# Layer-0 feed-forward finished batch by batch, and the causal maxima of layer 1 split between two stages

## The chip, the cores and the metric

One core of one Trainium2 chip runs the whole kernel as one launch. The metric is the device time of that launch in microseconds (us). Engines: PE is TensorE, DVE is VectorE, ACT is ScalarE, POOL is GpSimd, SP is SyncE, which here issues DMAs.

## The reference

Two transformer layers on x of 2 batches x 512 rows x 256 columns, all in float32. Each layer is

```python
h = layernorm(x) * (1 + ca) + sa
x = x + ga * attention(h)
h = layernorm(x) * (1 + cb) + sb
x = x + gb * ffn(h)
```

where the shifts, scales and gates are `silu(c) @ wmod`, per batch. Layer 0 has local attention (16 heads of 16, each query sees the 64 keys before it and itself) and a feed-forward part of one shared expert and 16 routed ones (top 4 of two groups). Layer 1 has causal attention:

```python
q = (h @ Wq.T + bq)            # 16 heads of 16
k = h @ Wk.T + bk              # one head of keys and of values for all
v = h @ Wv.T + bv
scores = where(k_pos < q_pos, q k^T / 4, NEG_BIG)
out = softmax(scores) @ v @ Wo.T + bo
```

and a feed-forward part of a shared expert of 1024 and 8 routed ones (top 2).

## The kernel before

**Arithmetic.** Every float32 product that needs the precision is made of float32r passes: an operand is split in a high part (ACT copies it to float32r) and a low part (DVE or POOL subtracts), and PE multiplies high x high, low x high and high x low (`product`, L553).

**Layer-0 feed-forward.** The hidden width is cut in 25 tiles of 128. A *unit* is one tile for one batch, 50 units in all. A unit is an up product `up` (L553: two halves g and u of six matmuls each, in PSUM banks 4 and 5), silu of g on ACT (L1308), g times u on DVE (L1783), times the routing weight (L1786), the high part on ACT (L1312), the low part on DVE (L1790) and the down product `down` (L994, twelve matmuls into the batch's two banks, 0 and 1 or 2 and 3, which gather the sum over all tiles). PE runs up(u), down(u-1), up(u+1) and so on. Units alternate between the batches, tile by tile, but for the last three tiles (`TAIL`): these are done for batch 0 and then for batch 1. Each tile's weights come by one DMA of 384 KB (`load_ffn`) into one of two raw buffers, ACT makes their high part (L1288), POOL their low part (L519, `weights_low`), into two pairs of tiles, `fwR`.

**Between the layers.** `half_out` (DVE) gates the summed output and adds it to x, with the statistics of the next norm; `norm_scales` and `normalise` follow, eight PE transposes (`norm_transposes`), `modulate` and `h_high` on ACT, `h_low` on DVE. Then `project1(b, m)` gives the queries (m = 0, 1), keys (2) and values (3) of layer 1; ACT adds the bias and makes high parts (`take_q1`), DVE low parts (`q1_low`). For this, `filler` puts matmuls without use into PE's stream (8 + 6 + 6 + 4 of them).

**Causal maxima.** Softmax needs each query's maximum over its keys before the scores are made again the other way round. For each of 32 heads (16 per batch) ACT masks the queries (`mask_q`, L1160), PE makes the scores (`scores`, L724 and the mask L729) in three banks, as three *pieces*, and DVE takes three maxima (`maxima`, L1572). Two groups of three banks alternate. The maxima go to DRAM (`store_maxima`, through SP) and come back as rows of the query operand in `qk_slot` (`load_keys_major`). All 32 heads are done before the next stage; the projections of batch 1 and the gates of layer 1 (`gates1`, L590) stand between the first ones.

**Values.** `keys_major(1, j)`, j = 0 to 47, makes scores with keys as rows for a third of the work of a pair of heads (L846, masks L852 and L855), in one of three pairs of banks; ACT takes the exponential (L1228); `values` (L877) multiplies with the values, one step late by a *quad* of four heads, which is six j; DVE turns and divides the result (`outputs`, L1588 to L1605). `values_pass(1)` runs over both batches without a break; the output projection of batch 0 (L892) stands in quads 5 and 6, and the norm transposes of batch 0 ahead of the last quad's values. The layer-1 feed-forward follows.

The order on each engine is the order of the code; nothing is scheduled by a program.

## Time and profile before

| what | value |
|---|---|
| three runs | 650.33, 648.99, 645.38 us |
| median | 648.99 us |
| span of the profiled execution, first to last instruction | 648.5 us |
| PE, DVE, ACT, POOL busy | 599.5, 379.0, 302.4, 118.5 us |
| mean granted clock of PE | 0.982 of 2.4 GHz |
| chain that ended last | PE 67%, DVE 19%, ACT 6% |

The profiler's execution is told by its span alone; no separate time of it is given. The span lies within 0.1% of the median of the runs, so that a sum made on the span can be read as one on the median. A clock of 1.00 in the rows is the level of 2.4 GHz, 0.50 that of 1.2 GHz; a value in between is a mean over a stretch that has both.

### The profile page before, as it was taken

Reading aid. Unit: us, or ns where it says so; the run is one execution under the profiler, and the core shown is the slowest. Engines: PE = TensorE matmul, PEld = TensorE weight load, DVE = VectorE, ACT = ScalarE, POOL = GpSimd, SP = SyncE. Lnnn points to the kernel's source line nnn. Section 1 sums busy time; section 2 is a strip of 40 time slices with the busy share of each in tenths; the row PEclk is TensorE's granted clock in tenths of the full one; section 3 lists DMA queues with packets and bytes.
Section 4 is the critical chain, followed back from the end, with each engine's and each line's share of the span. In section 5 each row is a group of like instructions: output and inputs, shape, how many; then the busy total and the mean of one; then the engine's idle time right before and its main releaser. Section 6 shows DMA issues by size and latency. Waiting matters only on the chain.

```text
span 648.5 us, 10714 instructions
## 1 busy us (share of the span) xinstructions
PE 599.5 (92%) x3880; PEld 470.2 (73%) x3890; DVE 379.0 (58%) x757; ACT 302.4 (47%) x466; POOL 118.5 (18%) x90
## 2 busy tenths in 40 slices
PE   3899999898999999999999797889999999999995
PEld 3778645786888888888887565544446878888885
DVE  7567757753254544454457799795376543335556
ACT  3666775463233333333342583448855643333331
POOL 4500031223022222112230000001301231222220
PEclk9998999999699999999999899899999999999999
DMA  8454674000011111111100024402310000111101
GB/s 319 123 213 135 221 215 132 1 25 24 2 36 42 45 49 49 49 49 49 49 25 1 0 71 134 127 4 77 113 40 1 25 25 25 50 49 49 48 2 65
DMA packets 22195, 44.66 MB, mean 69 GB/s; under 512 B 3632, under 2 KB 7632, under 8 KB 22160
## 3 DMA queue, kind: packets, MB, share of 16 engines
q1 hardware_dynamic: 21840, 44.05, 21.5%
q8 instruction: 23, 0.38, 0.2%
q10 hardware_dynamic: 320, 0.13, 0.1%
q14 instruction: 12, 0.10, 0.0%
HBM read 33.16 MB, written 11.01 MB: 68 GB/s over the span
## 4 chain that ended last, share of the span: by engine, by line
PE 67%; DVE 19%; ACT 6%; issue 3%; DMA 3%; POOL 1%; SPq 1%; DVEq 0%; ACTq 0%
PE PS L553 32%; PE PS L994 15%; DVE nmx L1572 5%; PE PS L877 4%; DMA qk_slot<-rows_scr 2%; PE PS L846 2%; PE PS L825 2%; PE PS L830 2%; DVE stats L1470 1%; PE PS L724 1%; DVE x L1641 1%; DVE xn L1786 1%; PE PS L892 1%; PE PS L713 1%; PE PS L561 1%
## 5 line engine op out<-in xcount | busy, mean ns | idle before, releaser
L1312 ACT ACTIVATE qk_hi<-xn 128x512 fp32r<-128x512 f32 x82 | 51.7, 631 | 170.5 <-DVE xn L1786 140.8
L553 PE MATMUL PS<-h_hi,wqkv_hi 128*128 128x512 f32 x304 | 104.4, 401 | 2.6 <-DVE h_lo L1504 1.9
L553 PE MATMUL PS<-h_hi,wqkv_lo 128*128 128x512 f32 x272 | 92.3, 395 | 1.8 <-DVE xn L1696 1.8
L1783 DVE TENSOR_TENSOR prs<-prs,PS 128x512 f32<-128x512 f32 x60 | 41.2, 687 | 88.7 <-PE PS L553 77.7
L519 POOL TENSOR_TENSOR wqkv_hi<-fw_raw,wqkv_hi 128x768 fp32r<-128x768 f32 x18 | 33.1, 1841 | 254.3 <-ACT wqkv_hi L1288 254.3
L1790 DVE TENSOR_TENSOR qk_lo<-xn,qk_hi 128x512 fp32r<-128x512 f32 x70 | 48.4, 692 | 49.1 <-ACT qk_hi L1312 49.1
L1308 ACT ACTIVATE prs<-PS 128x512 f32<-128x512 f32 x82 | 48.5, 592 | 47.3 <-PE PS L553 47.3
L553 PEld LDWEIGHTS PS<-h_hi,wqkv_hi 128*128 128x128 f32 x304 | 58.1, 191 | 15.3 <-DVE h_lo L1504 2.7
L553 PE MATMUL PS<-h_lo,wqkv_hi 128*128 128x512 f32 x160 | 63.6, 397 | 0.0
L553 PEld LDWEIGHTS PS<-h_hi,wqkv_lo 128*128 128x128 f32 x272 | 51.1, 188 | 13.3 <-DVE xn L1696 2.7
L1572 DVE TENSOR_REDUCE nmx<-PS 128x512 f32 (+4 forms) x96 | 54.2, 635 | 4.6 <-PE PS L729 4.5
L994 PE MATMUL PS<-wqkv_hi,qk_hi 128*128 128x256 f32 x280 | 52.1, 285 | 0.9 <-POOL qk_lo L525 0.7
L519 POOL TENSOR_TENSOR wqkv_lo<-fw_raw,wqkv_lo 128x768 fp32r<-128x768 f32 x16 | 29.5, 1846 | 122.4 <-ACT wqkv_lo L1288 122.4
L553 PE MATMUL PS<-h_lo,wqkv_lo 128*128 128x512 f32 x128 | 50.3, 393 | 0.0
L994 PEld LDWEIGHTS PS<-wqkv_hi,qk_hi 128*128 128x128 f32 x280 | 45.0, 188 | 5.0 <-POOL qk_lo L525 1.6
L994 PE MATMUL PS<-wqkv_lo,qk_hi 128*128 128x256 f32 x256 | 47.3, 283 | 0.7 <-DVE qk_lo L1790 0.7
L1786 DVE TENSOR_TENSOR xn<-prs,V 128x512 f32<-128x512 f32 x60 | 44.7, 745 | 2.1
L994 PEld LDWEIGHTS PS<-wqkv_lo,qk_hi 128*128 128x128 f32 x256 | 41.0, 188 | 4.0 <-DVE qk_lo L1790 1.5
L994 PE MATMUL PS<-wqkv_hi,qk_lo 128*128 128x256 f32 x140 | 39.5, 282 | 0.0
L1566 DVE TENSOR_REDUCE nmx<-PS 128x384 f32 (+1 forms) x64 | 31.1, 548 | 13.0 <-PE PS L713 12.9
L994 PE MATMUL PS<-wqkv_lo,qk_lo 128*128 128x256 f32 x128 | 36.0, 281 | 0.0
L1160 ACT ACTIVATE q_masked<-qk_hi,headmask 128x512 fp32r<-128x512 f32 (+1 forms) x48 | 32.3, 715 | 5.5 <-PE PS L729 3.5
(259 smaller groups left out, 1203.2 us busy)
## 6 DMA issues: line engine op xcount, KB each, us to landing
fw_raw<-in_ffn SPq DMA_DIRECT2D x41, 384.0 KB, 3.1
qk_slot<-rows_scr SPq DMA_DIRECT2D x32, 200.0 KB
rows_scr<-qk_hi SPq DMA_DIRECT2D x16, 256.0 KB
qk_slot<-q_scr SPq DMA_DIRECT2D x32, 100.0 KB
rows_scr<-qk_lo SPq DMA_DIRECT2D x8, 256.0 KB
wmod<-in_wmod SPq DMA_DIRECT2D x1, 1536.0 KB, 13.4
x<-in_x SPq DMA_DIRECT2D x2, 512.0 KB, 4.1
wmod<-in_wmod SPq DMA_DIRECT2D x1, 1024.0 KB, 9.6
```

The source lines that it names most:

```text
L519: nc.gpsimd.tensor_tensor(w[1], fw[s][:, :], w[0].bitcast(F32), ALU.subtract)\
L553: ins = nc.tensor.matmul(dst, left(a, c), right(b, c), start=n == 0, stop=n == total - 1)
L877: ins = nc.tensor.matmul(PS[s * VW:s * VW + rows, O_BANK[l][g % 2], kb * P:kb * P + n], v, probs[l][slot][:, col:col + n], start=kb == 0, ...
L994: ins = nc.tensor.matmul(PS[:, 2 * b + t // 2, (t % 2) * D:(t % 2 + 1) * D], hidR[u % 2 if isinstance(u, int) else b][a][:, t * P:(t + 1) ...
L1160: nc.scalar.activation(qm[s][:, :], rows[:, bass.ds(head // 2, 1), :].rearrange("p m t -> p (m t)").bitcast(F32), ACT.Copy, scale=headmask ...
L1308: nc.scalar.activation(gact[b], PS[:, 4, :], ACT.Silu).then_inc(f["silu"], 1)
L1312: nc.scalar.activation(hidR[b][0], hid[b], ACT.Copy).then_inc(f["hi"], 1)
L1566: nc.vector.tensor_reduce(nmx[:, bass.ds(NT * u + 2 * i, 2)], PS[:, 2 * h + i, 0:2 * KEYS0].rearrange("p (t k) -> p t k", k=KEYS0), X, ALU ...
L1572: nc.vector.tensor_reduce(nmx[:, bass.ds(NT * u + qt, k)], PS[:, 3 * h + bank, 0:k * w].rearrange("p (t k) -> p t k", k=w), X, ALU.max, ne ...
L1783: tt(hid[buf] if half is None else gu[buf], gact[buf], PS[:, 5, :], ALU.mult).then_inc(f["gu"], 1)
L1786: tt(hid[buf], gu[buf], cB[b][half], ALU.mult).then_inc(f["hid"], 1)
L1790: tt(hidR[buf][1], hid[buf], hidR[buf][0].bitcast(F32), ALU.subtract).then_inc(f["lo"], 1)
```

## The change

1. The layer-0 feed-forward runs its first 18 tiles by alternating batches, then the last seven tiles (`TAIL0`) for batch 0 and then for batch 1. It is written out without a loop. Weights have four pairs of tiles in place of two (and three more for the tail); ACT makes a tile's high part two tiles ahead of its use, right behind the silu of a unit instead of at the unit's end (`SPLIT0`).
2. During batch 1's seven units, batch 0 goes through `half_out`, the norm, the transposes, `modulate`, and its four layer-1 projections. The gates of layer 1 and their DVE steps go to the feed-forward's units 9 to 13. The fillers of this region are gone.
3. The causal maxima of batch 0 stand beside batch 1's norm and projections, with five banks in turn. Of batch 1, four heads (`AHEAD`) follow at once; the other twelve are cut in 36 pieces, two behind each `keys_major(1, j)` for j = 2 to 19 of batch 0's values, in three banks.
4. The values pass runs per batch (`values_pass1`), without overlap between the batches. Its scores have two pairs of banks in place of three (`PAIR_BANK`), so that `keys_major(1, j)` waits for the exponential of j - 2. The second store of maxima moves from ACT's queue to SP's, behind batch 0's loads.
5. The output projection of batch 0 stands at j = 30, its norm transposes at j = 39, `modulate` and `h_high` on ACT behind j = 40.

The core of the diff:

```diff
-TAIL = [3, 2]
+TAIL = 2
+TAIL0 = 7
+LAST0 = 2 * TILES[0]
+APART0 = TILES[0] - TAIL0
+TURN = LAST0 - TAIL0
+SCORE1 = [(0, 1, 6, 4, 5), (2, 3, 7)]
+PAIR_BANK = [0, 4]
+AHEAD = 4
+        fw0R = [fwR[0], fwR[1], fwX, fwE[1]]
...
+        SPLIT0 = {2 * APART0 - 4: APART0, 2 * APART0 - 3: APART0 + 1, 2 * APART0 - 1: APART0 + 2,
+                  **{2 * APART0 + k: APART0 + 2 + k for k in range(1, 5)},
+                  **{2 * i - 4: i for i in range(EARLY + 2, APART0)}}
...
+        def pieces_at(j):
+
+            first = 3 * AHEAD + 2 * (j - 2)
+            return [(n // 3, n % 3) for n in (first, first + 1) if 3 * AHEAD <= n < 3 * H]
...
             sp.wait_ge(ff[0]["split"], TILES[0])
             for s in range(2):
                 load_ffn(1, 0, s, s)
             store_maxima(sp, 1, 0)
-            sp.wait_ge(at[0]["st"], UNITS)
-            load_attention(1)
+            load_attention(1, 0, H)
+            store_maxima(sp, 1, 1)
+            load_attention(1, H, UNITS)
...
-                if u >= THIRDS:
-                    pe.wait_ge(a["p"], u - THIRDS + 1)
+                if u >= 2:
+                    pe.wait_ge(a["p"], u - 1)
+                if u == 0:
+                    pe.wait_ge(k1_loaded, 16 * 4)
+                    pe.wait_ge(a["mxd"], 3 * H)
+                elif u == THIRDS * PAIRS // 2:
+                    pe.wait_ge(k1_loaded, 16 * 4 * B)
+                    pe.wait_ge(a["mxd"], 3 * UNITS)
+                    pe.wait_ge(a["mlo"], B)
...
+            def beside_ffn0(u):
+
+                if u == EU + 1:
+                    pe.wait_ge(cB_ready, HALVES[0] * B)
+                    shifts1()
+                elif u == EU + 3:
+                    pe.wait_ge(shifts1_taken, 1)
+                    gates1(0)
+                    gates1(1)
+                elif u == TURN + 3:
+                    norm_transposes(2, (0,))
+                elif u == TURN + 4:
+                    project1(0, 2)
+                elif u == TURN + 5:
+                    project1(0, 3)
+                    project1(0, 0)
+                elif u == TURN + 6:
+                    project1(0, 1)
+
+            def ffn0():
+
+                early_ffn(0)
+                combine_table(0, 1)
+                for u in range(EU + 1, LAST0):
+                    b, i = unit0(u)
+                    up(0, u, b, weights(0, i), i)
+                    b, i = unit0(u - 1)
+                    down(0, u - 1, (u - 1) % 2, b, weights(0, i))
+                    beside_ffn0(u)
+                down_apart(0, LAST0 - 1, 1, weights(0, TILES[0] - 1))
...
+                    elif u == TURN:
+                        first = half_out(0, 0, 0)
+                        last = half_out(0, 0, 1)
+                    elif u == TURN + 1:
+                        first()
+                        last()
+                        norm_scales(2, slice(0, 1))
+                    elif u == TURN + 4:
+                        h_low(2, 0)
...
+                q1_low(0, 0)
+                first = half_out(0, 1, 0)
+                last = half_out(0, 1, 1)
+                first()
+                last()
+                norm_scales(2, slice(1, B))
+                normalise(2, 1)
+                q1_low(0, 1)
...
+                for i in range(H):
+                    maxima1(1, i)
+                    if i == 9:
+                        outputs(1, 0)
+                    elif i == 13:
+                        outputs(1, 1)
+                max_low(1, 1)
+                outputs(1, 2)
+                outputs(1, 3)
+                add_output_bias()
...
+            def values_pass1(b, beside):
+
+                first = b * THIRDS * PAIRS // 2
+                for j in range(first, first + 6):
+                    keys_major(1, j)
+                    beside(j)
+                for g in range(b * BQ + 1, (b + 1) * BQ):
+                    keys_major(1, 6 * g)
+                    beside(6 * g)
+                    keys_major(1, 6 * g + 1)
+                    beside(6 * g + 1)
+                    for kb in range(NT):
+                        values(1, g - 1, (kb,))
+                        keys_major(1, 6 * g + 2 + kb)
+                        beside(6 * g + 2 + kb)
+                values(1, (b + 1) * BQ - 1, range(NT))
```

How the instructions stand now, at three places. On PE at the end of the layer-0 feed-forward, before: the first row is the low part of the last but one down product, `o_parts` holds batch 0's normalised x, `wkv` the key and value weights.

```order
L1039 MATMUL PS<-qk_hi,qk_lo 128x256 x4
L696 MATMUL PS<-maskB,zeroB 128x512 x8
L631 MATMUL PS<-ident,o_parts 128x128 x8
L1034 MATMUL PS<-q_masked,qk_hi 128x256 x8
L1039 MATMUL PS<-q_masked,qk_lo 128x256 x4
L682 MATMUL PS<-hF,wkv 128x512 x2
L687 MATMUL PS<-wkv,hF 128x16 x8
```

The same place on PE now: from the end of down(47) to the first product of the last unit, whose weights are in `qk_slot` (`wq` are the query weights of layer 1).

```order
L1078 MATMUL PS<-prx_r,qk_lo 128x256
L748 MATMUL PS<-wkv,hF 128x16 x8
L616 MATMUL PS<-h_hi,wq_hi 128x512
L616 MATMUL PS<-h_lo,wq_hi 128x512
L616 MATMUL PS<-h_hi,wq_lo 128x512
L616 MATMUL PS<-h_hi,wq_hi 128x512
L616 MATMUL PS<-h_lo,wq_hi 128x512
L616 MATMUL PS<-h_hi,wq_lo 128x512
L616 MATMUL PS<-h_hi,qk_slot 128x512
```

The value and query projections of batch 0 stand between two units of batch 1; the fillers are gone, and so are the transposes between the last two down products.

On DVE, in the last units of batch 1, now (`h_lo` is batch 0's low part for the layer-1 norm, `wmod_r` its low part of the queries and keys, `V` its values; the last two rows are batch 1's output):

```order
L2009 TENSOR_TENSOR qk_lo<-xn,qk_hi 128x512
L1668 TENSOR_TENSOR h_lo<-hF,h_hi 128x512 x2
L2002 TENSOR_TENSOR prs<-prs,PS 128x512
L2005 TENSOR_TENSOR xn<-prs,V 128x512
L2009 TENSOR_TENSOR qk_lo<-xn,qk_hi 128x512
L1862 TENSOR_TENSOR wmod_r<-w_raw,wmod_r 128x512
L1867 TENSOR_TENSOR V<-PS,bv 128x4x16
L2002 TENSOR_TENSOR prs<-prs,PS 128x512
L2005 TENSOR_TENSOR xn<-prs,V 128x512
L2009 TENSOR_TENSOR qk_lo<-xn,qk_hi 128x512
L1862 TENSOR_TENSOR wmod_r<-w_raw,wmod_r 128x512
L1809 TENSOR_TENSOR xn<-PS,gate 128x512
```

Before, the rows of `h_lo` and the low parts stood behind the last output (L1639) and ahead of the first maximum (L1572); batch 1's output and norm still stand ahead of the first maximum (L1741).

On PE in the values, before, with keys (L846), masks (L855) and values (L877) in turn:

```order
L846 MATMUL PS<-qk_slot,k 128x256 x2
L855 MATMUL PS<-maskB,identB 128x128 x2
L877 MATMUL PS<-prs,V 32x384 x2
L877 MATMUL PS<-prx,V 32x384 x2
L846 MATMUL PS<-qk_slot,k 128x512 x2
L855 MATMUL PS<-maskB,identB 128x128 x2
```

The same place now, in batch 0's pass:

```order
L879 MATMUL PS<-qk_slot,k 128x256 x2
L888 MATMUL PS<-maskB,identB 128x128 x2
L789 MATMUL PS<-wqkv_hi,q_masked 128x256 x2
L794 MATMUL PS<-maskB,identB 128x256
L794 MATMUL PS<-maskB,identB 128x128
L789 MATMUL PS<-wqkv_hi,q_masked 128x384
L794 MATMUL PS<-maskB,identB 128x128
L910 MATMUL PS<-prs,V 32x384 x2
L910 MATMUL PS<-prx,V 32x384 x2
L879 MATMUL PS<-qk_slot,k 128x512 x2
L888 MATMUL PS<-maskB,identB 128x128 x2
```

Two pieces of a head of batch 1 (L789 and its masks) have come between a keys step and the values.

## Rows read from the trace of the kernel before

**Rows 1.** By stretch: busy us (xcount) of PE, PEld, DVE, ACT, POOL; clock; DMA; GB/s.
```profile
360.40:373.30 12.90, 10.76 (x51) 7.18 (x52) 10.32 (x34) 6.52 (x13) 0.00 (x0) 0.87 0.00 0
373.30:410.80 37.50, 33.13 (x210) 24.36 (x209) 37.11 (x67) 18.24 (x29) 0.00 (x0) 1.00 0.36 106
410.80:434.20 23.40, 17.54 (x101) 11.41 (x101) 19.34 (x36) 11.18 (x17) 0.00 (x0) 0.93 0.18 60
434.20:491.80 57.60, 56.58 (x514) 25.41 (x515) 31.06 (x68) 44.44 (x56) 9.39 (x6) 1.00 0.22 66
413.70:417.30 3.60, 3.59 (x14) 2.63 (x14) 2.01 (x4) 2.43 (x4) 0.00 (x0) 0.53 0.23 75
```
**Rows 2.** Waits from 360 to 434 us: total, times, longest.
```profile
PE PS L724 <- DVE nmx L1572: 7.6, 16, 1.0
```
**Rows 3.** Stretch of the maxima, DVE busy with L1572 alone.
```profile
373.30:434.20 60.90, 52.92 (x94) 0.97 0.29 89
```
**Rows 4.** Timeline of PE, first products of two heads in a row.
```profile
418.92 0.50 PE L724 MATMUL PS<-wqkv_hi,q_masked 128*128 128x256 f32 x2 [0.23 <-DVE nmx L1572]
...
420.58 0.50 PE L724 MATMUL PS<-wqkv_hi,q_masked 128*128 128x256 f32 x2 [0.40 <-DVE nmx L1572]
```
**Rows 5.** Chain that ended last, layer-0 feed-forward: start, us, what.
```profile
256.25 2.78 PE PS L553 x12
259.03 1.43 PE PS L994 x12
```
**Rows 6.** Timeline of PE in layer 1's values, two quads apart.
```profile
446.80 1.07 PE L877 MATMUL PS<-wmod,V 128*32 128x512 f32 x8
...
459.98 1.06 PE L877 MATMUL PS<-wmod,V 128*32 128x512 f32 x8
```
**Rows 7.** Timeline of PE at the end of that feed-forward.
```profile
353.70 0.64 PE L1039 MATMUL PS<-qk_hi,qk_lo 128*128 128x256 f32 x4
...
357.93 1.09 PE L631 MATMUL PS<-ident,o_parts 128*128 128x128 f32 x8 [1.84 <-ACT o_parts L1124]
...
359.80 0.64 PE L1039 MATMUL PS<-q_masked,qk_lo 128*128 128x256 f32 x4
```
**Rows 8.** Timeline of PE among the maxima: key and value projection, gates.
```profile
378.22 1.94 PE L682 MATMUL PS<-hF,wkv 128*128 128x512 f32 x4
...
389.91 1.91 PE L687 MATMUL PS<-wkv,hF 128*128 128x16 f32 x16
...
405.14 1.95 PE L590 MATMUL PS<-wmod,o_parts 128*128 128x256 f32 x8
```
**Rows 9.** Timeline of DVE: batch 1's output, batch 0's low parts, batch 1's norm.
```profile
360.48 0.69 DVE L1639 TENSOR_TENSOR xn<-PS,gate 128x512 f32<-128x512 f32 x1 [1.36 <-PE PS L1039]
...
364.99 1.26 DVE L1504 TENSOR_TENSOR h_lo<-hF,h_hi 128x512 fp32r<-128x512 f32 x2
...
368.54 1.38 DVE L1498 TENSOR_SCALAR xn<-x,mv,rs 128x256 f32<-128x256 f32 x4
```
**Rows 10.** Timeline of SP's queue, the store of maxima and the loads behind it.
```profile
412.74 0.57 SPq L304 DMA_DIRECT2D q_scr<-mxT_hi  x1
...
415.25 37.47 SPq L372 DMA_DIRECT2D qk_slot<-q_scr  x20
```
**Rows 11.** Chain that ended last, layer 0: a load of rows behind others.
```profile
74.61 7.86 DMA qk_slot<-rows_scr
```
**Rows 12.** Timeline of ACT: modulation of batch 0 and its high parts.
```profile
490.72 1.43 ACT L1134 ACTIVATE hF<-PS,modT 128x512 f32<-128x512 f32 x2
492.05 1.14 ACT L1141 ACTIVATE h_hi<-hF 128x512 fp32r<-128x512 f32 x2
```
**Rows 13.** Timeline of PE: batch 1's last output projection in layer 1.
```profile
498.12 0.39 PE L892 MATMUL PS<-wout_hi,qk_hi 128*128 128x256 f32 x1 [1.01 <-POOL qk_lo L496]
```
**Rows 14.** Timelines of POOL, DVE and PE around 327 us: one weight split.
```profile
327.13 1.85 POOL L519 TENSOR_TENSOR qk_lo<-fw_raw,qk_hi 128x768 fp32r<-128x768 f32 x1
...
327.27 2.26 DVE L1786 TENSOR_TENSOR xn<-prs,V 128x512 f32<-128x512 f32 x1
...
330.98 0.51 PE L994 MATMUL PS<-wqkv_lo,qk_hi 128*128 128x256 f32 x2 [0.32 <-DVE qk_lo L1790]
```

More of the change, by code:

```diff
@@ new lines, in up @@
+            def up(l, u, b, w, tile, halves=(0, 1)):
+                f = ff[l]
+                ge(f["split"], tile + 1)
+                for i in halves:
+                    if i == 0:
+                        ge(f["silu"], u)
+                    elif isinstance(u, int) and u <= EU:
+                        ge(f["early_hid"], u)
+                    else:
+                        ge(f["gu"], u - EU)
+                    product(PS[:, 4 + i, :], lambda a, c: w[a][:, i * D + c * P:i * D + (c + 1) * P],
+                            lambda a, c: hR[a][:, c, b, :], KC).then_inc(f[("g", "u")[i]], 1)
```

968 lines of the change are left out of this document (516 added, 452 removed).

## The prediction

> **What bounds the kernel now.** I read the busy time by stretch first, for the stage that is rebuilt, then the waits, then the timelines of PE and DVE at its borders. All times are of the profiled execution, whose span is 648.5 us. The changed region goes from 354 us, near the end of layer 0's feed-forward, to 498 us; what lies outside is untouched. The stretches show who sets the pace [rows 1]. From 360.4 to 373.3 (batch 1's output, norm and first projections) no engine is full: the work passes from one to the other. From 373.3 to 410.8 DVE is busy 37.1 of 37.5 us and PE 33.1. From 410.8 to 434.2 DVE has 19.3 of 23.4. Then, in the values, PE has 56.6 of 57.6 us and DVE only 31.1. The waits agree: PE stood 7.6 us for the maxima, in 16 waits [rows 2]. So the maxima are paid at DVE's rate in one stage, and DVE is half idle in the next, where PE is full. The change moves twelve of 32 heads there, and it moves batch 0's norm and projections into the feed-forward, where PE is also full. Each move trades a DVE microsecond for a PE one. The question is what is left.
>
> **Prices.** The 94 recorded maxima are 52.9 us [rows 3], so 0.56 us each and 1.7 us a head of three. One head takes PE 1.66 us from start to start, 0.40 of it a wait [rows 4], so at most 1.26; without the tail of its last matmul I take 1.17. A feed-forward unit is 2.78 + 1.43 = 4.21 us of PE [rows 5], and six of the twelve up matmuls, the size of a query projection, are 1.4. A quad of the values is (459.98 - 446.80) / 2 = 6.59 us of PE [rows 6].
>
> **Step 1, the end of the feed-forward.** Before, the last but one down product ended at 353.70 + 0.64 = 354.3 and the last at 359.80 + 0.64 = 360.4 [rows 7]; between stood fillers, a wait of 1.84 and the transposes. Without them the last would end at 354.3 + 1.4 = 355.7. But PE now does more here: the gates, two groups of eight (1.95 with the tail, some 1.65 alone) 3.3; keys 1.4 (of 1.94) and values 1.8 (of 1.91) [rows 8]; two query projections 2.8 [rows 5]; eight transposes 1.0 [rows 7]. Together 10.3: 366.0. The DVE work of batch 0's output and norm falls between units: two gated halves, 4.5 us (360.48 to 364.99), and some 2.4 of small steps ahead of 368.54 [rows 9]. A unit needs 2.1 us of DVE in 4.21, so it catches up in about three units, and g times u of the next two comes late. I count four waits of PE of 0.7, less what stood there before: 2 us. End of the last down product: 368.0, 7.6 later than before.
>
> **Step 2, to batch 0's first values.** From here DVE sets the pace again. Batch 1's output and norm stand ahead of the first maximum, in DVE's order: 360.48 to 369.92 was 9.4 [rows 9], less batch 0's 1.2 of low parts, plus one low part of 0.7: 9.0. Everything behind it (all maxima, and PE's scores once five banks are full) waits for that. Then 16 heads, 16 x 1.67 = 26.7, with 3.3 of low parts and values between: 30. PE has four projections of batch 1 behind heads 5 to 8, 5.9 us on top of four heads at 1.17, 10.6 in all, against 6.7 us of DVE and five pieces (2.8) of lead: 1.1 of wait, and 1.4 more for the clock, which falls in the idle 7 us before (below). So the last maximum of batch 0 ends 41.3 us after the down product. The first values then wait for two things. PE and DVE do four heads of batch 1, 6.5 us. Beside it runs the chain: PE and ACT turn the maxima, 0.8; from the store's issue to the first load's 2.5 (412.74 to 415.25 [rows 10]); then the landing of the first pair. The trace shows no such landing alone: nothing is the lower bound, 7.9 the upper, a load in layer 0 behind much traffic [rows 11]. I take 4.5, between them, since eight loads and two weight tiles share the queue. 0.8 + 2.5 + 4.5 = 7.8. So the first keys step comes at 368.0 + 41.3 + 7.8 = 417.1, against 434.2 [rows 1]: 17.1 us earlier.
>
> **Step 3, the values.** They took 57.6 us [rows 1]; the work in it stays. Added: twelve heads of PE, 12 x 1.17 = 14.0. DVE has 12 x 1.67 = 20 us and two outputs in some 33 us, and has room, but an output between heads 13 and 14 (six instructions, at the 0.46 us of the stretch's mean, 31.06 over 68, some 2.8 us [rows 1]) holds PE 1.3, as three banks hold one head. At the border of the batches nothing overlaps: the last quad's values wait for the last exponential (1.0), and the first six keys steps of batch 1 wait for exponentials in turn, with two pairs of banks (1.8 more than in a quad). The second store and load of maxima gives 1.5 to 4 us of wait against the 2.9 us of values and exponential that cover it: 2.0. Two pairs of banks in the other quads: an exponential is 0.8 us on the mean (44.44 over 56 [rows 1]) and up to 1.0, and has to fit between two keys steps; some 0.3 a quad, 1.0. `modulate` and the high parts, 1.43 + 1.14 [rows 12], stand before an exponential at j = 40; with two pairs of banks PE is held 2.2. One old wait of 0.7 goes. Sum: 57.6 + 14.0 + 1.3 + 2.8 + 2.0 + 1.0 + 2.2 - 0.7 = 80.2. End 417.1 + 80.2 = 497.3, against 491.8: 5.5 later.
>
> **Step 4, layer 1's feed-forward.** Its first product waited for batch 0's low parts, and batch 1's last output projection until 498.12, 6.3 behind the values and 1.01 of it idle, for an output on DVE that stood behind those low parts [rows 13]. Now the low parts are long done. The output projection comes 4.6 us after the values, not 6.3, and what follows it starts 2 us or so earlier: -2.2.
>
> **Sum.** 5.5 - 2.2 = +3.3 on 648.5: 651.8, and with the median 0.5 above the span and the waits rounded up, 651.5 on either. A measurement of this kernel can tell about 1% (6.5 us) from no change: this is none. The ends of the unknown costs: the waits that I added are 2.0 + 2.5 + 4.5 of landing less 3.2 hidden + 1.3 + 2.8 + 2.0 + 1.0 + 2.2 = 15.1. With a third of them it is 641.5; with landings of 7.9 at both borders (3.4 each), 658.
>
> **Two rules, weighed.** The row at 327 us shows a multiplication of DVE on SBUF tiles (L1786) of 2.26 us, where others are 0.69, beside a split of POOL of 1.85; PE then waited 0.32 [rows 14]. The Trainium skill (SBUF — State Buffer, SBUF: two separate sides) says that a DVE instruction with two SBUF inputs and GpSimd share a port pair under an exclusive lock, and the later one stands for the whole instruction. By that rule the split, which now starts right behind a silu, falls on that multiplication in every tile; the trace agrees for the one case that it has. It makes the second rival below.
>
> The stretch from 413.7 had PE busy 3.59 of 3.60 us at a granted clock of 0.53, the 1.2 GHz level, after 2 us of idling, with 14 matmuls in 3.6 us, so 2.05 a head of eight [rows 1]. The Trainium skill (TensorE: Matmul & The Clock Gate, Loop structure matters more than you think) says that matmuls behind a long wait run cold. That speaks against removing the fillers and standing 7 us ahead of the maxima; it is the first rival.
>
> **Rivals.**
> 1. *Slower by the clock.* PE idles 7 us ahead of the maxima and then runs at 1.2 GHz beside DVE. A head is 2.05, not 1.67: over 16 heads 6.1, and the 5.9 of projections double: +12 less the 1.4 counted, 662. It decides if the clock stays down for more than some 4 us after the restart. Against it: once PE is behind, it is full, and in the last of [rows 1] it was back after 3.6 us. Chance 0.14.
> 2. *Slower by the port.* Each of 18 later splits costs PE 0.32 as at 327 us [rows 14]: 5.8, 657. It decides where the low part comes more than 0.4 us later than I reckon. Chance 0.12.
> 3. *Faster, the borders close.* The waits of the values are the weakest part of my sum: if PE's order leaves just enough between a keys step and its exponential, and the landings are short, 10 of the 15.1 us go: 641.5. For it: in layer 0 the same two pairs of banks are used. Chance 0.24.
> 4. *The overlap fails.* Rows for the values land as late as in [rows 11] at both borders, DVE and PE both standing: +6.8, 658. Chance 0.08.
>
> My forecast has 0.42. Within 1% lie it and a little of 2 and 3: same 0.46; faster 0.23; slower 0.31. The range reaches from rival 3 with some more gone to rival 1: 639 to 662.
>
> **What would show it.** Right: PE without a wait over 1 us through the feed-forward's last 14 units, last down product near 368; then 7 us of PE idle; the first keys step near 417; maxima beside values with DVE under 80% busy; batch 1's pass near 34 us with waits for exponentials. Wrong: the first keys step before 413 or behind 421, a granted clock of 0.5 beyond 5 us in the maxima, long L1786-type multiplications in each second unit, or a pass of batch 0 over 48 us.

## The result, and the profile after

The changed kernel took 661.6 us (median of four runs, 657.8 to 664.9) against 649.7 us for the kernel before on the same chip (median of four runs, 645.4 to 658.9): a ratio of 1.019, 95% interval 1.013 to 1.026. A run more than 1.5% above the fastest of its kernel is left out of the ratios, the intervals and the mean clocks in this document, but not out of the medians. Run again beside the experiments it gave 660.4 us and 1.015 (1.007 to 1.023). I had forecast 651.5 us and no difference that can be told. The profiled execution has a span of 663.1 us, 14.6 more than before, and a mean granted clock of 0.961 against 0.982.

A stage at a time (windows of the changed kernel; start:end, length, busy time and instructions of PE, PEld, DVE, ACT and POOL, granted clock, DMA share, GB/s):

```profile
368.60:377.50 8.90, 1.71 (x14) 1.13 (x12) 8.27 (x29) 3.70 (x6) 0.00 (x0) 0.73 0.26 73
377.50:418.10 40.60, 34.00 (x189) 23.78 (x189) 36.52 (x66) 19.06 (x29) 0.00 (x0) 0.89 0.35 104
418.10:463.50 45.40, 41.35 (x339) 22.34 (x337) 28.77 (x53) 26.18 (x34) 1.26 (x1) 0.96 0.11 38
463.50:507.80 44.30, 39.56 (x273) 18.92 (x274) 21.26 (x50) 26.18 (x33) 9.35 (x5) 0.75 0.19 58
507.80:663.10 155.30, 146.85 (x848) 127.10 (x848) 74.91 (x130) 57.81 (x93) 33.50 (x20) 0.99 0.11 35
```

The first row is batch 1's norm behind the last down product, the second the maxima up to the first keys step, the third and fourth the values of batch 0 and of batch 1, the last all that follows. In the values before, PE was busy 56.6 of 57.6 us at a clock of 1.00 [rows 1]. Now they last 45.4 + 44.3 = 89.7 us, and in batch 1's the clock is 0.75: half of that stretch ran at 1.2 GHz.

Against the kernel before: the first keys step comes 16.1 us earlier (418.1 for 434.2), the values last 32.1 us longer (89.7 for 57.6), and what follows is 1.4 us shorter (155.3 for 156.7). The sum is the 14.6. My forecast for the three was -17.1, +22.6 and -2.2.

PE's timeline at the places that matter (start, duration, line, operation, tiles, shape, count, idle time before and what ended it):

```profile
367.96 0.64 PE L1094 MATMUL PS<-qk_slot,qk_lo 128*128 128x256 f32 x4
378.30 0.80 PE L789 MATMUL PS<-wmod_r,q_masked 128*128 128x512 f32 x1 [7.99 <-DVE nmx L1741]
418.10 0.50 PE L879 MATMUL PS<-qk_slot,k 50*128 50x512 f32 x2
444.81 0.50 PE L879 MATMUL PS<-qk_slot,k 50*128 50x384 f32 x4
450.53 0.47 PE L789 MATMUL PS<-wqkv_hi,q_masked 128*128 128x256 f32 x2 [1.61 <-DVE nmx L1741]
451.11 0.80 PE L879 MATMUL PS<-qk_slot,k 50*128 50x384 f32 x4
460.15 2.36 PE L910 MATMUL PS<-wmod,V 128*32 128x512 f32 x32 [0.81 <-ACT wmod L1344]
463.51 0.50 PE L879 MATMUL PS<-qk_slot,k 50*128 50x512 f32 x2 [1.00 <-DMA qk_slot<-q_scr]
465.41 0.39 PE L879 MATMUL PS<-qk_slot,k 50*128 50x256 f32 x2 [0.41 <-ACT prs L1344]
492.27 0.80 PE L879 MATMUL PS<-qk_slot,k 50*128 50x384 f32 x4 [2.06 <-ACT prx L1344]
503.29 4.50 PE L910 MATMUL PS<-wmod,V 128*32 128x512 f32 x32 [0.78 <-ACT wmod L1344]
```

Two pairs in it show the clock without any clock column. The same four matmuls of a keys step took 0.50 us at 444.8 and 0.80 at 451.1 and 492.3; the same 32 matmuls of a batch's last quad took 2.36 us at 460.2 and 4.50 at 503.3. The stretches between such rows:

```profile
378.30:382.70 4.40, 4.40 (x20) 3.52 (x20) 3.35 (x6) 2.35 (x4) 0.00 (x0) 0.50 0.55 182
450.50:454.90 4.40, 4.37 (x22) 2.09 (x22) 2.79 (x5) 1.02 (x1) 0.62 (x1) 0.61 0.00 0
468.25:475.13 6.88, 6.78 (x31) 5.89 (x32) 3.04 (x5) 3.17 (x4) 1.83 (x1) 0.51 0.29 86
492.27:508.80 16.53, 15.75 (x92) 5.67 (x93) 3.85 (x6) 7.24 (x9) 3.28 (x2) 0.50 0.08 25
```

The last three lie in the values and just behind them. Each is full of PE work (the third has one wait of 0.78 us in it), and each stands behind waits: 1.61 us ahead of the first, 0.81, 1.00 and three of some 0.4 ahead of the second, 2.06 ahead of the third. At full clock the same work would take less by the missing share: 4.40 x 0.39 + 6.88 x 0.49 + 16.53 x 0.50 = 13.4 us, if nothing else held PE there. That is more than the whole miss of 11.3 us (a span of 663.1 for 651.8), so it was the first theory (A). Its rival (B) was that the hand-overs through two pairs of banks set the pace, so that a faster PE would only wait longer.

### The profile page after: what moved, and what is told of

Same layout as the page of the kernel before. It is cut to its first block, busy times and chain, and to the rows that moved or that the text cites. A ratio compares the mean times of both kernels' runs of the same rounds, so it can differ in the third digit from the quotient of the medians.

```text
span 663.1 us, 10265 instructions
## 1 busy us (share of the span) xinstructions
PE 607.7 (92%) x3866; PEld 474.1 (71%) x3866; DVE 395.5 (60%) x757; ACT 302.2 (46%) x466; POOL 120.3 (18%) x90
## 4 chain that ended last, share of the span: by engine, by line
PE 71%; DVE 17%; ACT 5%; DMA 2%; issue 2%; POOL 1%; SPq 0%; ACTq 0%; DVEq 0%
PE PS L616 31%; PE PS L1078 15%; PE PS L910 4%; DVE nmx L1741 3%; PE PS L879 2%; PE PS L789 2%; PE PS L772 2%; PE PS L770 2%; PE PS L850 2%; PE PS L925 2%; PE PS L855 2%; DVE xn L2005 1%; DVE stats L1634 1%; DMA qk_slot<-rows_scr 1%; DVE x L1811 1%
## 5 line engine op out<-in xcount | busy, mean ns | idle before, releaser
L616 PE MATMUL PS<-h_hi,wqkv_hi 128*128 128x512 f32 x224 | 78.1, 405 | 3.3 <-DVE h_lo L1668 1.9
L616 PE MATMUL PS<-h_hi,wqkv_lo 128*128 128x512 f32 x208 | 71.9, 399 | 2.2 <-DVE xn L1917 1.8
L1741 DVE TENSOR_REDUCE nmx<-PS 128x2 f32<-128x512 f32 (+2 forms) x96 | 56.0, 641 | 13.0 <-PE PS L794 12.6
L2005 DVE TENSOR_TENSOR xn<-prs,V 128x512 f32<-128x512 f32 x60 | 61.4, 1024 | 2.1
L616 PEld LDWEIGHTS PS<-h_hi,wqkv_hi 128*128 128x128 f32 x224 | 43.1, 193 | 13.1 <-DVE h_lo L1668 2.5
L616 PE MATMUL PS<-h_lo,wqkv_hi 128*128 128x512 f32 x120 | 48.3, 403 | 0.0
L1078 PE MATMUL PS<-wqkv_hi,qk_hi 128*128 128x256 f32 x200 | 37.7, 287 | 1.9 <-DVE qk_lo L2009 1.2
L576 POOL TENSOR_TENSOR wqkv_lo<-fw_raw,wqkv_lo 128x768 fp32r<-128x768 f32 x12 | 22.6, 1880 | 85.1 <-ACT wqkv_lo L1403 85.1
L1078 PEld LDWEIGHTS PS<-wqkv_hi,qk_hi 128*128 128x128 f32 x200 | 31.7, 188 | 6.0 <-DVE qk_lo L2009 2.9
L789 PE MATMUL PS<-wmod_r,q_masked 128*128 128x256 f32 (+1 forms) x64 | 21.8, 416 | 10.9 <-DVE nmx L1741 10.9
L1344 ACT ACTIVATE wmod<-PS 128x1024 f32<-128x1024 f32 (+1 forms) x24 | 20.8, 882 | 21.5 <-PE PS L885 11.0
```

The lines of the kernel that those rows point to most:

```text
L576: nc.gpsimd.tensor_tensor(w[1], fw[s][:, :], w[0].bitcast(F32), ALU.subtract)\
L616: ins = nc.tensor.matmul(dst, left(a, c), right(b, c), start=n == 0, stop=n == total - 1)
L789: nc.tensor.matmul(PS[:, scored1(b, i, piece), col:col + WIDTH1[qt]], qm[s][:, qt * P:(qt + 1) * P], q1R[b][0][:, 2, 0:WIDTH1[qt]], start= ...
L1078: ins = nc.tensor.matmul(PS[:, 2 * b + t // 2, (t % 2) * D:(t % 2 + 1) * D], hidR[buf][a][:, t * P:(t + 1) * P], w[v][:, 2 * D:], start=Fa ...
L1741: nc.vector.tensor_reduce(nmx[:, NT * u + qt:NT * u + qt + k], PS[:, scored1(b, i, piece), 0:k * w].rearrange("p (t k) -> p t k", k=w), X, ...
L2005: tt(hid[buf], gu[buf], cB[b][half], ALU.mult).then_inc(f["hid"], 1)
```

## The experiments

Each ratio is to the kernel before, run beside the experiment. A *filler* or "zeros" means matmuls on zeros whose result nobody reads. With each run stands its mean granted clock over the whole kernel.

### First round: what holds the clock, and what the two moves are worth

**e1_fill.** Matmuls on zeros, with no reader, in PE's waits:

```diff
+            FILL = {24: 4, 25: 1, 26: 2, 27: 2, 28: 1, 29: 2, 36: 1, 42: 1, 43: 9, 'end0': 4, 'end1': 4}
+
+            def fill(j):
+
+                if j == 36:
+                    pe.wait_ge(y_gated, 5 * B)
+                if j in FILL:
+                    filler(FILL[j], 3)
...
                 for i, piece in pieces_at(j):
+                    if (i, piece) == (15, 0):
+                        pe.wait_ge(at[1]["oe"], 2)
+                        filler(6, 6)
                     scores1(1, i, (piece,))
```

> The changed kernel plus matmuls on zeros that nobody reads, put only where PE stood in its values passes: 6 ahead of the last head's first score (it waited 1.6 us there), 4 and 4 at the border of the batches, 1 or 2 ahead of each keys step that waited, 9 ahead of the keys step that waited 2.06 us at 490, 4 ahead of the last values. Theory A, the clock: the 10 us by which the values passes missed my forecast are stretches at the 1.2 GHz level behind short waits (450.5 to 454.9, 468.3 to 475.1, 492.3 to 508.8, some 13 us of loss). Then these matmuls, though they are more work, hold the granted clock near 1.00 from 450 to 509, the pass of batch 1 (463.5 to 507.8, 44.3 us) falls to 34 to 37 us, and the time to 649 to 654 us. Rival B, the hand-over: two pairs of banks make PE wait for each exponential, and a faster PE only waits longer. Then the time stays at 659 to 664 us, and the pass stays over 42 us with waits for exponentials in place of long matmuls.

Measured: 658.9 us (651.5 to 662.4, four runs), ratio 1.014 (1.009 to 1.019): behind the 649 to 654 of A, just under the 659 of B, and not to be told from the change. The profiled run is the 651.5. Its two passes (windows):

```profile
415.20:459.00 43.80, 42.85 (x353) 22.70 (x351) 28.61 (x53) 26.20 (x34) 1.26 (x1) 1.00 0.11 35
459.00:495.00 36.00, 35.13 (x297) 16.70 (x297) 22.23 (x50) 25.96 (x33) 9.21 (x5) 1.00 0.23 71
```

and its last values (timeline of PE):

```profile
492.60 2.36 PE L910 MATMUL PS<-wmod,V 128*32 128x512 f32 x32
```

PE does 37 matmuls more and the passes are 9.9 us shorter, with a clock of 1.00 throughout. In this run A's mechanism is seen, and its time; but the other three runs had clocks of 0.969 to 0.980 and 656 to 661 us of span. Whether they lost their clock in the values is not known.

**e2_mod.** The modulation of batch 0's second norm on DVE:

```diff
                 elif j == 40:
-                    modulate(3, 0)
                     h_high(3, 0)
...
                 outputs(1, BQ)
+                dve.wait_ge(xt_ready, 7)
+                for c in range(KC):
+                    ts(hF[:, c, 0, :], PS[:, XT_BANK[3][0][c], :], modT[:, 1, 6 + c, 0:1], modT[:, 1, 4 + c, 0:1],
+                       ALU.mult, ALU.add).then_inc(h_ready[0], 1)
                 outputs(1, BQ + 1)
```

> The changed kernel with the modulation of layer 1's second norm of batch 0 (two ACT instructions, 1.44 us) on DVE, which idles then, so that the exponential behind it comes sooner and PE's wait of 2.06 us at 490 shrinks to 0.6 or less. Theory A: the clock does not fall there, so the 16 us from 492.3 to 508.8 run at 2.4 GHz: 1.5 for the wait and 6 to 8 for the clock, 652 to 655 us. Rival B: only the wait goes, 659 to 661 us.

Measured: 660.6 us (ten runs, 652.2 to 670.0), ratio 1.011 (1.007 to 1.015). The ratio is made of six of the ten runs, whose median is 656.8. Neither is in A's 652 to 655, and the median of all lies in B's 659 to 661. In the profiled run (657.6 us) the wait is 0.72 us, and the clock behind it did not fall (timeline of PE, then the two passes as windows):

```profile
491.94 0.50 PE L879 MATMUL PS<-qk_slot,k 50*128 50x384 f32 x4 [0.72 <-ACT prx L1344]
498.75 2.36 PE L910 MATMUL PS<-wmod,V 128*32 128x512 f32 x32 [0.80 <-ACT wmod L1344]
```

```profile
418.30:463.50 45.20, 41.30 (x338) 22.00 (x337) 28.57 (x52) 26.21 (x34) 1.26 (x1) 0.96 0.11 32
463.50:501.10 37.60, 34.20 (x273) 17.89 (x274) 23.02 (x53) 24.68 (x31) 9.24 (x5) 0.86 0.21 68
```

Batch 1's pass went from 44.3 to 37.6 us for one wait that is 1.3 us shorter; the pass of batch 0, untouched, is as in the change. So the profile speaks for A and the medians do not. The ten runs show why one of them says little: their spans lie near one line against the clock, from 650.4 us at 0.980 over 655.8 at 0.970 and 660.7 at 0.963 to 668.1 at 0.953, some 6 us for each 0.01. A 0.01 of 655 us is 13 us spent at half clock, so 6.5 us of loss where PE is full. One program gives a spread of clocks; that the waits shift this spread is what the second round is to show.

**e3_ahead16.** All maxima ahead of the values:

```diff
-AHEAD = 4
+AHEAD = 16
...
                     maxima1(1, i)
-                    if i == 9:
-                        outputs(1, 0)
-                    elif i == 13:
-                        outputs(1, 1)
+                outputs(1, 0)
+                outputs(1, 1)
                 max_low(1, 1)
```

> The changed kernel with all 16 heads of batch 1's maxima ahead of the values and none beside them, all else kept (border, two pairs of banks, the work moved into the feed-forward). By my prices: 12 heads at DVE's rate of 1.67 put 20.0 us ahead of the first keys step (near 438); out of batch 0's pass go 14.0 of PE, the 1.6 us wait at 449 and 2.2 of slow clock behind it, so it takes 27 to 29 us instead of 45.4. Sum +2: 662 to 665 us, the overlap worth about 2 us only. Rival: the pieces of scores between keys steps cost more than their PE time (they open the waits that drop the clock in the rest); then the time falls to 650 to 657 us.

Measured: 675.3 us, 1.036 (1.031 to 1.040): worse than either end of what I expected. The profile:

```profile
377.50:442.85 65.35, 54.36 (x284) 35.24 (x285) 59.46 (x106) 25.56 (x38) 0.00 (x0) 0.90 0.25 77
442.85:468.00 25.15, 24.02 (x134) 8.78 (x134) 2.55 (x5) 13.52 (x16) 0.00 (x0) 0.59 0.11 33
468.00:480.60 12.60, 10.66 (x113) 4.59 (x113) 4.96 (x11) 7.13 (x10) 1.27 (x1) 1.00 0.11 33
```

The maxima stage grew by 24.8 us, not 20.0; batch 1's heads have three banks, and the last ones came 1.82 us apart (435.69, 437.51, 439.33), not 1.67, which is 1.8 of the 4.8 (the rest I did not trace). Batch 0's pass took 25.15 + 12.60 = 37.75 us, of which 25.15 x 0.41 = 10.3 are the slow clock; the other 27.4 are what I had priced (27 to 29). Ahead of the fall stood two waits of 0.36 and 0.40 us, behind a long stage at DVE's pace in which PE waits some 0.15 us in each head. So the overlap is worth more than my 2 us, about 14 us of median in this pair. Part of that is the clock: this pass loses 10.3 us to it where the change's own loses 1.8 (0.04 of 45.4), but the mean clocks of all runs, 0.956 and 0.967, make it some 7 us over the whole kernel. The rival, that the time falls to 650 to 657 us because the pieces open the waits which drop the clock, is out.

**e4_late.** Batch 0's transposes, modulation and four projections behind the feed-forward instead of in it (the same calls, moved on PE, ACT and DVE):

```diff
-                elif u == TURN + 3:
-                    norm_transposes(2, (0,))
-                elif u == TURN + 4:
-                    project1(0, 2)
...
+                norm_transposes(2, (0,))
+                for m in (2, 3, 0, 1):
+                    project1(0, m)
                 pe.wait_ge(qhi, 4 * B + 2)
```

> The changed kernel with batch 0's norm transposes, modulation, and four projections of layer 1 taken out of the feed-forward and put right behind its last down product, where PE stood 8.0 us for batch 1's norm on DVE. Theory C, PE time was what counted: the last down product comes 7 to 9 us earlier (360 to 362 instead of 368.6), PE has 7.0 us of work in the idle stretch and the chain from transposes to the first score is 10 to 12 us against the 9.0 of DVE's norm; all later stages come 5 to 7 us earlier: 653 to 657 us. My step 1 had this move as a gain: by that rival the chain and DVE's order add 9 us or more behind the last down product and the time stays at 660 us or rises.

Measured: 662.0 us, 1.018 (1.014 to 1.022), the same as the change and not the 653 to 657 of theory C. On DVE (timeline):

```profile
368.57 0.69 DVE L1854 TENSOR_TENSOR wmod_r<-w_raw,wmod_r 128x512 fp32r<-128x512 f32 x1 [0.16 <-ACT wmod_r L1530]
371.60 0.69 DVE L1854 TENSOR_TENSOR wmod_r<-w_raw,wmod_r 128x512 fp32r<-128x512 f32 x1 [2.20 <-ACT wmod_r L1530]
376.95 0.69 DVE L1854 TENSOR_TENSOR wmod_r<-w_raw,wmod_r 128x512 fp32r<-128x512 f32 x1 [0.97 <-ACT wmod_r L1530]
377.56 1.75 DVE L1733 TENSOR_REDUCE nmx<-PS 128x2 f32<-128x512 f32 x3
```

The last down product ended at 362.6, 6.0 earlier, and the first maximum began at 377.56, where it began in the change (377.55). DVE now stands 2.20 and 0.97 us for low parts whose projections come late. The rival holds for the whole package. What the change moved into the feed-forward cost 6 us of PE there and won 6 us of chain behind it.

### Second round: the repairs together, no border, and a wait planted in the kernel before

**f1_fillmod.** Both edits of above (3 zeros instead of 9 at step 43).

> The changed kernel with both repairs of the first round: matmuls on zeros where PE stood in the values (now 3 instead of 9 at the keys step after the modulation) and the modulation on DVE. The first round's timed runs line up on the clock: with the modulation on DVE, ten runs gave 650.4 us of span at a mean granted clock of 0.980 and 668.1 at 0.953, 6.5 us for each 0.01. Theory A: with fewer waits more runs hold the clock; mean clock 0.978 to 0.985 in most runs, median 650 to 655 us. Rival B (waits themselves, not the clock): the two gave 3 and 1 us of median; together 656 to 659 us whatever the clock.

Measured: 654.5 us (eleven runs, 651.0 to 661.2), 1.005 (1.001 to 1.009), mean clock 0.978 for the change's 0.967. This is 6 to 7 us under the change, by work that computes nothing and one modulation on another engine; the wait that the modulation takes away accounts for some 1.3 of it. The median is A's; B's 656 to 659 us lies just outside the interval of the ratio (650.9 to 655.9 us).

**f2_noborder.** The three pieces of a head beside one keys step, and batch 1's keys among batch 0's last values:

```diff
-            first = 3 * AHEAD + 2 * (j - 2)
-            return [(n // 3, n % 3) for n in (first, first + 1) if 3 * AHEAD <= n < 3 * H]
+            i = AHEAD + j - 2
+            return [(i, n) for n in range(3)] if AHEAD <= i < H else []
...
-                if j == 21:
+                if j == 15:
                     max_rows(1, 1)
...
-                values_pass1(0, beside_first_values)
-                values_pass1(1, beside_last_values)
+                values_pass1()
```

> The changed kernel without a border between the batches' values: three pieces of batch 1's maxima beside each keys step from the third on (two before), so that they are stored by the 16th step, and batch 1's keys steps run among batch 0's last values; the output projection, the norm and the modulation of batch 0 are placed as in the kernel before. What I priced at the border was 2.8 + 2.0 and at the modulation 2.2, less 2 that the tail got from the early norm. Theory A: 5 to 6 us of waits go (passes from first keys to last values 83 us or less against 89.7), the clock does not fall at 450 to 475, mean clock 0.975 or more: 650 to 654 us. Rival B: PE is held at DVE's rate in the first steps instead (3 x 0.56 us a step, against 1.1 to 1.9 of PE), the first pass grows by what the border saved: 659 to 664 us.

Measured: 653.7 us (ten runs), 1.005 (1.001 to 1.008), mean clock 0.975: in A's range, and B's 659 to 664 is out. The profiled run (span 646.9, clock 0.983), first keys step to last values:

```profile
417.70:491.00 73.30, 70.58 (x612) 35.71 (x611) 51.15 (x101) 50.65 (x65) 9.77 (x6) 1.00 0.19 59
```

73.3 us where the change took 89.7. The clock stands at 1.00, as in e1_fill's 79.8; the 6.5 us between the two I put down to the waits of the border and the modulation, which e1_fill filled and this kernel does not have. DVE's rate did not hold PE: the longest wait for a maximum is 0.68 us. In the profiled run this kernel is below the kernel before; over ten runs it is not, at a mean clock of 0.975 for that kernel's 0.983.

**f4_before_wait.** The kernel before, with one wait and nothing else:

```diff
             def keys_major(l, u):
                 a = at[l]
+                if (l, u) == (1, 43):
+                    pe.wait_ge(a["p"], 43)
...
+                if j == 42:
+                    for i in range(5):
+                        nc.scalar.activation(table_in[:, :], ct[:, 0, 0, 0:1], ACT.Exp).then_inc(act_order, 1)
+                        act.wait_ge(act_order, 2 + i)
```

> The kernel before, with one wait put into its values: PE waits at keys step 43 for the exponential just before it, and ACT does five tiny activations (0.2 us each) ahead of that exponential. PE then stands some 2 to 2.5 us once, as in the changed kernel at 490. Theory A (one wait of 2 us drops the clock for what follows): the time rises by 6 to 10 us over the kernel before, with long matmuls behind the wait, 655 to 660 us. Rival B: it rises by the wait alone, 2 us, 651 to 653 us, granted clock unchanged.

Measured: 654.6 us (ten runs), 1.006 (1.003 to 1.009), so 4.0 us (1.8 to 6.1) over the kernel before, mean clock 0.978 for its 0.983. Two rows of PE's timeline, and two windows:

```profile
485.46 0.51 PE L848 MATMUL PS<-qk_slot,k 50*128 50x384 f32 x4 [2.35 <-ACT wmod L1234]
491.76 0.80 PE L848 MATMUL PS<-qk_slot,k 50*128 50x384 f32 x4
```

```profile
485.00:490.00 5.00, 4.54 (x28) 1.48 (x28) 3.68 (x8) 2.03 (x3) 1.37 (x1) 0.70 0.00 0
490.00:495.00 5.00, 5.00 (x34) 2.34 (x33) 1.11 (x3) 2.49 (x3) 0.00 (x0) 0.50 0.00 0
```

A kernel that has none of the change's machinery loses its clock behind one wait of 2.35 us, and has it back at about 497, after 10 us. That is 5 us of loss, and with the wait some 7, which is what this run pays (a span of 655.1 for 648.5). So the mechanism is A's. The median pays 4.0, under the 6 to 10 that I expected; the profiled run is at the top of its ten, and what the others lost behind the wait is not to be seen. By the time alone B's 2 us is not quite out, since the interval starts at 1.8; by the clock it is, as B had it unchanged and it went from 0.983 to 0.978 in the mean of ten runs.

**c_after.** The change again.

> The changed kernel once more, unchanged, beside the others on the same chip. Theory A: its runs lie on the same line of span against mean clock (663.1 at 0.961, 655.9 at 0.973), and in its profile the stretches at 1.2 GHz stand behind waits of PE in the values, though not the same ones as in the first profile need fall. Rival B: the stretches at 1.2 GHz differ and the time does not. 656 to 664 us.

Measured: 660.4 us. Its profile (span 661.2, clock 0.967) has the slow stretches at the same two places, behind the border and behind step 43. The one at 450 is missing this time, though the wait of 1.61 us is there, and a new one stands in layer 0 (below). The line of span against clock is loose here: 655.8 us at 0.978 and 655.9 at 0.968.

### Third round: what is left, and a version below both

**h1_swap** (run last) is f2_noborder with one order changed:

```diff
-                max_rows(1, 0)
                 pe.wait_ge(qhi, 4 * B + 6)
                 pe.wait_ge(v1_taken, 2)
-                for i in range(AHEAD):
+                scores1(1, 0)
+                max_rows(1, 0)
+                for i in range(1, AHEAD):
                     scores1(1, i)
```

**g1_fill8** has this and 22 zeros in the 8 us that PE idles ahead of the maxima; **g2_lateq** has this and three projections of batch 0 moved out of the feed-forward into that stretch; **g3_lateq_fill** has all, with 9 zeros. The first piece below is of g1_fill8, the rest of g2_lateq:

```diff
+                        scores1(0, 1, (0, 1))
+                        pe.wait_ge(y_gated, 2 * B * 2)
+                        filler(22, 3)
+                        scores1(0, 1, (2,))
...
-                elif u == TURN + 5:
-                    project1(0, 3)
-                    project1(0, 0)
-                elif u == TURN + 6:
-                    project1(0, 1)
...
+                for m in (0, 3, 1):
+                    project1(0, m)
                 pe.wait_ge(qhi, 4 * B + 2)
```

> The borderless kernel of the second round, with 22 matmuls on zeros in the 8.0 us in which PE stands ahead of the maxima, and batch 1's first head scored ahead of the transposition of batch 0's maxima (PE waited 2.1 us there). Of what is left between the borderless kernel (653.7) and the kernel before (650.2), theory A says: it is again the clock, in the maxima (0.61 from 370 to 380 and 0.83 to 0.87 in two later stretches of its profile). With the 8 us filled the granted clock stays at 1.00 from 370 to 390, DVE's waits of 0.9 and 0.3 us ahead of the second and third head go, mean clock up by 0.003 to 0.006 though most of that is beside DVE: 650 to 653 us. Rival B: DVE sets the pace there whatever the clock: no change, 653 to 655 us.

> The borderless kernel with the same swap of the transposition, and with three of the four projections of batch 0 that the change put into the feed-forward (both queries and the values, 4.6 us of PE) moved behind the last down product, into PE's idle 8 us; the norm, modulation and key projection stay in the feed-forward. Theory C: PE time in the feed-forward is on the path and DVE's 9 us behind it hide the projections, at 1.2 us more on DVE (values taken, one low part): the last down product 4.6 us earlier (near 364), the first maximum 3 to 4 us earlier, time 649 to 651.5 us. Rival: as when all was moved out (first maximum unchanged at 377.6): the chain from the query projection to the first score is longer than DVE's norm; no change, 653 to 655 us.

> The same as the one with three late projections, plus 9 matmuls on zeros in what is left of PE's idle stretch. If both the clock and the place of the projections count: 647.5 to 650.5 us, level with or below the kernel before (650.2), PE without a wait over 2 us from 360 to 490 and the granted clock at 1.00 from 360 to 400. If neither: 653 to 655 us.

> The borderless kernel with the swap alone (batch 1's first head scored ahead of the transposition of batch 0's maxima), nothing in the idle 8 us, projections as in the change. It parts the 4.7 us between the borderless kernel (653.7 us, mean clock of ten runs 0.974) and the one with swap and filled idle stretch (649.0, 0.983). If the filled idle stretch held the clock: 652.5 to 654 us, mean clock of the runs 0.973 to 0.977. If the removed wait of 2.1 us did (it stood last ahead of the values): 648.5 to 650.5 us, mean clock 0.981 or more.

| kernel | median, us | ratio to before, 95% | mean clock |
|---|---|---|---|
| the change | 661.6, 660.4 | 1.019 (1.013 to 1.026), 1.015 (1.007 to 1.023) | 0.967 |
| f2_noborder | 653.7 | 1.005 (1.001 to 1.008) | 0.975 |
| h1_swap | 650.2 | 1.002 (0.999 to 1.006) | 0.979 |
| g1_fill8 | 649.0 | 0.997 (0.994 to 1.000) | 0.983 |
| g3_lateq_fill | 648.1 | 0.996 (0.992 to 0.9995) | 0.983 |
| g2_lateq | 647.3 | 0.995 (0.992 to 0.998) | 0.982 |
| the kernel before | 649.4 to 650.2 | 1 | 0.983 |

Of the 4.7 us between f2_noborder and g1_fill8 the swap alone has 3.5 by the medians, but only 0.24 of 0.78% by the ratios, whose intervals overlap; the mean clock went up by the same step each time. Neither of my two readings won outright. g1_fill8's median is below both of its ranges (650 to 653 and 653 to 655), g3_lateq_fill's is in the upper one of its two (647.5 to 650.5). g2_lateq met its expectation in the profile and passed it in the median (647.3 for 649 to 651.5). Its PE and DVE timelines at the first maxima, and the window of its values:

```profile
375.22 0.79 PE L789 MATMUL PS<-wmod_r,q_masked 128*128 128x512 f32 x1 [3.50 <-DVE nmx L1736]
```

```profile
374.49 3.40 DVE L1736 TENSOR_REDUCE nmx<-PS 128x2 f32<-128x512 f32 x6
```

```profile
416.40:489.70 73.30, 70.56 (x610) 35.78 (x611) 51.19 (x101) 50.70 (x65) 9.76 (x6) 1.00 0.17 54
```

Its last down product ends at 364.9 and the first maximum starts at 374.49, 3.1 us earlier than in the change. With the norm and the key projection left in the feed-forward, the chain behind the last down product is shorter than DVE's 9 us, and the other 4.6 us of PE hide beside it: 3.5 us of idling are left of 8.0. The further zeros of g3 bought nothing that these runs can tell. g2_lateq has the lowest median of the study, below the kernel before by 0.5% (0.2 to 0.8%), with g3_lateq_fill and g1_fill8 too near to be told from it; it keeps both ideas of the change and drops its border.

## Why the prediction was wrong

Step by step.

1. **The end of the feed-forward** was right: 368.0 forecast, 368.6 measured, with four waits of PE in batch 1's units that make 2.1 us (2 forecast), the longest 0.76. What I did not see is that the place of the projections was open: e4_late won nothing by moving all 7.0 us of PE behind the feed-forward, but g2_lateq shows that 4.6 of them fit in the idle stretch, with the first maximum 3.1 us earlier.
2. **The maxima** were right in sum: the first maximum 9.0 us behind the last down product (8.95 measured), the first keys step at 417.1 (418.1). In parts, batch 0's last maximum ended 42.5 us behind the down product (41.3 forecast; my terms, 9.0 + 30 + 1.1 + 1.4, add up to 41.5) and the keys step came 7.0 us after it (7.8). The landing of the rows, which I had as the last of the chain, was not: PE went from batch 1's heads to the keys step without a wait.
3. **The values** are the step that failed: 80.2 us forecast, 89.7 measured, 9.5 of the 11.3 us of miss. The waits in it were near their prices: 1.3 between heads 13 and 14 (1.61), 1.0 for the last exponential (0.81), 2.2 at the modulation (2.06), 2.0 for the second batch's rows (1.00); all of PE's waits listed there make 8.8 us, where my terms for waits make 9.3. What failed is that the sum counted each wait at its length and put the clock behind it at nothing. At a clock of 1.00 the two passes took 79.8 us in e1_fill, with zeros in the waits, so by that one profile the missing term is some 9.9 us. The 13.4 us from the rows is an upper bound for it, and I did not trace the difference.
4. **Layer 1's feed-forward**: -2.2 forecast, -1.4 measured.

The rows that I had put on record held the missing term. The stretch at a clock of 0.53 from 413.7 in the kernel before [rows 1] stands behind two waits that make 2.5 us (PE's timeline, before):

```profile
412.10 0.30 PE L747 MATMUL PS<-ident,nmx 128*64 128x128 f32 x1 [1.18 <-ACT gate L1116]
413.71 0.79 PE L724 MATMUL PS<-wqkv_hi,q_masked 128*128 128x256 f32 x2 [1.31 <-ACT q_masked L1160]
```

I used it for the 7 us of idling alone, and not for the 2.2 us that I put at the modulation.

**The rivals.** The first, the clock, had the right mechanism in the wrong place, and its 662 us met the measured 661.6 by accident. I let the clock fall behind the 7 us of idling ahead of the maxima. It did: 0.50 from 378.3 to 382.7, 4.4 us, where I had asked for some 4, and again from 403.5 for some 3 us. But there DVE sets the pace and a slow PE costs little: in the first fall DVE waited 1.2 us for scores, against the 1.4 in my sum, and the 16 heads' maxima took 33.6 us from first to last, against 33.2 in g1_fill8, where the clock was held at 1.00 through the idling and the first heads. Where PE is full, waits of 0.4 to 2 us were enough, and there I had counted each wait once. The Trainium skill (TensorE: Matmul & The Clock Gate, Loop structure matters more than you think) says that matmuls behind a long wait run cold; I read "long" as the 7 us, and the rows show it for 2.06 and 2.35 too.

The second rival, the port: the multiplication of DVE in the feed-forward is long in many tiles now,

```profile
L2005 DVE TENSOR_TENSOR xn<-prs,V 128x512 f32<-128x512 f32 x60 | 61.4, 1024 | 2.1
```

1024 ns in the mean where it was 745 (44.7 us over 60). Its mechanism came as the rival has it. In the feed-forward 18 of the multiplications take 1.50 to 2.26 us, each starts while a split of POOL runs, and each ends 0.55 us after the split does, within 0.01; no short one starts inside a split. One pair of the 18 (timelines of POOL and DVE):

```profile
249.34 1.85 POOL L576 TENSOR_TENSOR prx_r<-fw_raw,prx_r 128x768 fp32r<-128x768 f32 x1 [6.59 <-ACT prx_r L1403]
250.05 1.69 DVE L2005 TENSOR_TENSOR xn<-prs,V 128x512 f32<-128x512 f32 x1
```

Its price, 5.8 us of waits, did not come: from 164 to 337 us, where all 18 lie, PE waits for DVE once, 0.72 us at 313.3, and the last long multiplication ahead of that had ended 6.6 us before. That the splits are the cause is read from these times; no run moved them. The third (borders close) did not come. The fourth (rows land late) did not come either: 1.00 us at the border and no DMA wait ahead of the first keys step.

**What stays open.** Which of the unprofiled runs lost its clock where is not to be seen; only their means are known. Not all of it is lost in the values. f1_fillmod's profile has every stretch of the values at 1.00 and still a span of 656.8, because it ran at half clock for 16 us in layer 0's values, which no kernel here changes, behind a wait for rows. The window in f1_fillmod, then the same place in three timelines (f1_fillmod, c_after, the change):

```profile
81.50:97.50 16.00, 15.98 (x102) 6.31 (x106) 4.90 (x6) 6.60 (x9) 4.15 (x3) 0.50 0.50 149
```

```profile
81.52 0.82 PE L850 MATMUL PS<-maskB,identB 128*128 128x384 bf16 x2 [1.80 <-DMA qk_slot<-rows_scr]
82.93 0.82 PE L850 MATMUL PS<-maskB,identB 128*128 128x384 bf16 x2 [2.24 <-DMA qk_slot<-rows_scr]
82.98 0.50 PE L850 MATMUL PS<-maskB,identB 128*128 128x384 bf16 x2 [1.65 <-DMA qk_slot<-rows_scr]
```

In the 14 profiles this wait is 1.19 to 1.42 us nine times, with the clock at 1.00 to 100 us each time. It is 1.57 to 2.24 us five times, and in four of these the clock fell within some 3 us; only the change's own 1.65 was without effect. So a part of each kernel's spread of clocks comes from here and has nothing to do with the change. And the share of the swap and of the zeros in the last 4.7 us is not settled.

## What to carry to other kernels

Where PE sets the pace, price a wait at its length plus what the half clock behind it costs, and not only waits of many microseconds: here one of 2 us cost 4 us (1.8 to 6.1) in a kernel that was otherwise full, and in one profile of the change 16.5 us at half clock, a loss of 8, stood behind one of 2.06. Where another engine sets the pace the slow clock is nearly free, so ask which engine is full behind the wait before counting it. A pipeline that is cut in two (a border between passes, a side job ahead of the exponential that the next product waits for) can pay twice; keep the next batch's steps running across the border, and put side jobs on the engine that idles.

## What the hardware showed that I had not expected

The granted clock is a spread, not a number: e2_mod's ten runs had 0.953 to 0.980 in one session on one chip and the changed kernel's eight 0.957 to 0.978, while all 82 runs of the kernel before beside the experiments lie within 0.965 to 0.988, with means near 0.983. The change, which adds short waits to a stage with PE full, has a lower mean, 0.967. Two runs of one program can differ by 18 us (e2_mod), so one profile tells where a loss can be and not how large it is in the median. The same wait need not have the same effect: the clock fell behind the 1.61 us at 450 in one profile of the change and not in the other. And it fell behind waits that look harmless, 0.36 and 0.40 us in e3_ahead16, after which PE, busy 24.0 of 25.2 us, ran for 22 us mostly at 1.2 GHz before it was back.
